# Four graph layers in one kernel: border, layer order and query/key stacks rearranged

## What is computed

```python
# layer 0: mean over neighbours
agg = (adj @ x) / maximum(adj.sum(-1), 1e-6);  y0 = relu(concat([x, agg]) @ W.T)
# layer 1: attention-like transition, two hops
e = leaky_relu(sj[None, :] + si[:, None] + ab, 0.2);  a = adj * exp(e)
T = a / (a.sum(-1) + 1e-12);  y1 = relu(sum_k (T^k x) @ Wk[k] + bk[k])   # k = 0, 1, 2
# layer 2: three graph convolutions
h = relu(adj' @ (x @ W1) + b1); h = relu(adj' @ (h @ W2) + b2); y2 = adj' @ (h @ W3) + b3
# layer 3: 8 heads of 32, scores multiplied by 2 * adj before the softmax
s = (q @ k.T) * 32 ** -0.5 * (adj + adj);  y3 = softmax(s) @ v @ Wo.T + bo
# after each layer: x = layernorm(x + y)
```

## Time and profile before

| what | value |
|---|---|
| median of 3 runs | 3148.42 us |
| profiled execution | 3147.59 us |
| its span, first to last instruction | 3145.7 us |
| granted TensorE clock, mean | 0.993 |
| TensorE (PE) busy | 3023.7 us |
| DVE, ACT, POOL busy | 2083.8, 1724.0, 453.5 us |
| DMA, mean over the span | 75 GB/s |

### The profile page before, as it was taken

One profiled execution on the slowest core, in us unless ns is written; L12 is line 12 of the kernel. 1 busy time (PEld: TensorE's weight loads), 2 busy tenths in 40 slices (PEclk: granted clock), 3 DMA queues, 4 the chain that ended last, 5 costly groups with the idle time before them and its releaser, 6 DMA issues.

```text
span 3145.7 us, 71077 instructions
## 1 busy us (share of the span) xinstructions
PE 3023.7 (96%) x28188; PEld 2644.0 (84%) x28188; DVE 2083.8 (66%) x4020; ACT 1724.0 (55%) x3048; POOL 453.5 (14%) x1666
## 2 busy tenths in 40 slices
PE   6999999999999999999999999999999999999999
PEld 6988789887898778987789877898778987789877
DVE  5637976379762797627975289753887438874387
ACT  3525854258552684426844278542784327853377
POOL 0101211012110122101221012111121111211112
PEclk9999999999999999999999999999999999999999
DMA  5122131121321213202133021330213302133110
GB/s 218 36 72 69 45 145 54 57 70 45 142 77 37 66 52 135 90 28 66 49 135 108 11 72 42 135 108 14 68 51 125 108 14 72 50 124 108 28 39 19
DMA packets 145271, 234.50 MB, mean 75 GB/s; under 512 B 12840, under 2 KB 113965, under 8 KB 144941
## 3 DMA queue, kind: packets, MB, share of 16 engines
q1 hardware_dynamic: 144940, 229.96, 22.5%
HBM read 120.86 MB, written 83.89 MB: 65 GB/s over the span
## 4 chain that ended last, share of the span: by engine, by line
PE 80%; DVE 10%; ACT 3%; issue 2%; SPq 2%; POOL 2%; DMA 0%; DVEq 0%; POOLq 0%; ACTq 0%
PE ps L725 15%; PE ps L497 15%; PE ps L499 14%; PE ps L498 14%; PE ps L715 9%; PE ps L743 7%; DVE rsum L1280 2%; PE ps L598 2%; SPq L400 1%; PE ps L587 1%; PE ps L756 1%; DVE ev L1379 1%; PE ps L555 1%; DVE t_lo L1210 1%; POOL rstd L461 1%
## 5 line engine op out<-in xcount | busy, mean ns | idle before, releaser
L1466 DVE CUSTOM_DVE_ANT_0 r<-ps,adjn 128x1024 f32<-128x1024 f32 x512 | 620.7, 1212 | 19.5 <-DVE xr L1502 10.3
L1141 ACT ACTIVATE r<-r,nmax 128x1024 f32<-128x1024 f32 x512 | 584.9, 1142 | 23.0 <-POOL nmax L489 22.6
L497 PE MATMUL ps<-u_hi,t_hi 128*128 128x256 f32 x2048 | 589.9, 288 | 5.8 <-DVE u_lo L1190 4.8
L499 PE MATMUL ps<-u_hi,t_lo 128*128 128x256 f32 x2048 | 579.2, 283 | 0.0
L498 PE MATMUL ps<-u_lo,t_hi 128*128 128x256 f32 x2048 | 578.8, 283 | 0.0
L725 PEld LDWEIGHTS ps<-ident,r 128*128 128x128 f32 x4096 | 462.5, 141 | 115.4 <-issue 77.6
L725 PE MATMUL ps<-ident,r 128*128 128x128 f32 x4096 | 536.7, 274 | 7.3 <-DVE pt L1482 6.9
L1482 DVE COPY pt<-ps 128x512 f32<-128x512 f32 x512 | 352.9, 689 | 92.6 <-PE ps L725 75.0
L497 PEld LDWEIGHTS ps<-u_hi,t_hi 128*128 128x128 f32 x2048 | 391.2, 191 | 14.3 <-DVE t_lo L1190 7.7
L907 ACT ACTIVATE pt<-ps 128x512 f32<-128x512 f32 x512 | 304.0, 594 | 175.8 <-PE ps L725 161.9
L498 PEld LDWEIGHTS ps<-u_lo,t_hi 128*128 128x128 f32 x2048 | 391.1, 191 | 0.0
(11 more groups left out here) (162 smaller groups left out, 5233.9 us busy)
## 6 DMA issues: line engine op xcount, KB each, us to landing
adjn<-in_adj SPq DMA_DIRECT2D x64, 512.0 KB, 3.4
t_spill<-t_hi SPq DMA_DIRECT2D x64, 512.0 KB, 4.5
t_spill<-t_lo SPq DMA_DIRECT2D x64, 512.0 KB, 5.3
t_hi<-t_spill SPq DMA_DIRECT2D x32, 1024.0 KB, 5.3
t_lo<-t_spill SPq DMA_DIRECT2D x32, 1024.0 KB, 8.0
xn<-in_x SPq DMA_DIRECT2D x16, 512.0 KB, 4.5
x_spill<-xn SPq DMA_DIRECT2D x64, 128.0 KB, 1.7
q_stack<-u_hi SPq DMA_DIRECT2D x64, 128.0 KB, 2.4
```

Of the source, the lines that this page charges most:

```text
L497: pe.matmul(dst, a_hi, b_hi, start=first, stop=False, skip_group_check=check)
L499: return pe.matmul(dst, a_lo, b_hi, start=False, stop=last, skip_group_check=check)
L1141: act.activation(r[:, s % RSLOTS, :], r[:, s % RSLOTS, :], ACT.Exp, bias=nmax[:, s % 4:s % 4 + 1], accum_out=prow[:, qt % 2, h:h + 1]).the ...
L1466: dve.tensor_tensor_reduce(out=r[:, s % RSLOTS, :], in0=ps[:, 2 * (s % 2):2 * (s % 2) + 2, :].rearrange("p a c -> p (a c)"), in1=adjn[:, q ...
```

## The change

It has four parts.

1. *Border.* The first halves of block columns 0 to 3 of the next adj are transposed inside the loop of the element before: 8 transposes ahead of the last context group, 8 behind it. Their copies are put into the lists of ACT and DVE at the loop's end; one DVE piece stands between the last output's sum and its statistics. `spread_denominators` of the last tile comes earlier, the last context group uses another PSUM bank, and the last tile's `c_f`, `c_hi`, `c_lo` are made in two halves. The `g` projections alternate one by one with the adj columns.
2. *Degrees.* One reduction before the border, three ahead of layer 0, four between its tiles; the reciprocals in two halves.
3. *Layer 1.* `v` pairs 0 to 2 move ahead of the late x transposes and of `s_j(1)`, pair 3 behind the first alpha transpose; DVE makes both parts of all four; ACT writes the first half of `sj_row`; two of the `s_i` move down. The own part runs two tiles ahead in the second hop.
4. *Stacks.* Only heads 0 and 1 are stacked by TensorE, and not their second query halves: 6 copies. All else is moved by transfers of 32 partitions x 2 KB, query or key and half each by itself: per element 78. The order of the projections is changed to suit. The last projection comes behind `scores(0)`. `scores(u)` of heads 2 to 7 waits for the transfers of its head, `scores(32)` for the second query halves. The copies to `pt` wait in steps.

The diff, cut to what decides:

```diff
+    PLACED = 2
+    COPIES = [(h, m, half) for m, half in ((1, 0), (0, 0), (1, 1)) for h in range(PLACED)]
-    QK = [(1, 0, 0), (1, 1, 0), (0, 0, 0), (0, 1, 0), (1, 0, 1), (1, 1, 1), (0, 0, 1), (0, 1, 1)]
+    QK = [(0, 1, 0), (0, 0, 0), (1, 1, 0), (1, 0, 0), (0, 1, 1), (1, 1, 1), (0, 0, 1), (1, 0, 1)]
...
+        P_RING = ([(pt_0, k) for k in (2, 0, 6, 4, 3)] + [(pt_1, k) for k in range(6)] +
+                  [(pt_0, 1), (pt_0, 5), (pt_2, 0), (pt_2, 1)])
...   SyncE
-                for g in range(G):
-                    rows = slice(HD * g, HD * (g + 1))
-                    for n in range(2):
-                        if g == 0:
-                            sp.wait_ge(pr_free, nth(b, PR_UNITS, pr["qk", (1, n, 1)] + 1))
-                        at = slice(n * N, (n + 1) * N)
-                        hi, lo = f32(u_hi[rows, at]), f32(u_lo[rows, at])
-                        stack = q_stack if n == 0 else k_stack
-                        for part, src in enumerate((hi, hi, lo) if n == 0 else (lo, hi, hi)):
-                            sp.dma_start(f32(stack[HD * part:HD * (part + 1), G + g, :]), src).then_inc(stacked[g], 16)
+                def moved(h, m, half, signal):
+                    src_rows, at = slice(HD * (h % G), HD * (h % G + 1)), slice(half * 512, (half + 1) * 512)
+                    stack = (q_stack, k_stack)[m]
+                    for part, lo in enumerate((0, 0, 1) if m == 0 else (1, 0, 0)):
+                        sp.dma_start(f32(stack[HD * part:HD * (part + 1), h, at]),
+                                     f32(qk_place((h // G, m, half), lo)[src_rows, :])).then_inc(signal, 16)
...
+                part_done((0, 0, 0))
+                first_halves(range(PLACED, G))
+                part_done((1, 0, 0))
+                first_halves(range(G, G + 1))
+                part_done((0, 1, 1))
+                key_halves(range(PLACED, G))
+                first_halves(range(G + 1, H))
+                part_done((1, 1, 1))
+                key_halves(range(G, H))
+                part_done((1, 0, 1))
+                for g in (1, 0):
+                    for h in range(G * g, G * (g + 1)):
+                        moved(h, 0, 1, queries_in[g])
...   TensorE, scores
+                if u < PLACED:
+                    copied(b, len(COPIES) - PLACED + u)
+                elif u < H:
+                    wait_first(pe, b, (u,))
+                    wait_keys(pe, b, (u,))
+                if u == H * TPH:
+                    wait_queries(pe, b, 0)
+                    wait_queries(pe, b, 1)
...   TensorE, query/key phase
+                qk_part(4)
+                for n in range(2 * PLACED):
                     stack_copies(b, n)
+                qk_part(5)
+                for n in range(2 * PLACED, 3 * PLACED):
+                    stack_copies(b, n)
+                qk_part(6)
                 scores(b, 0)
+                qk_part(7)
...   TensorE, end of the loop
+                    if s in (UNITS + 1, UNITS + 5) and b + 1 < B:
+                        for j in ((0, 1) if s == UNITS + 1 else (2, 3)):
+                            transpose_adj(b + 1, j, 0)
...   TensorE, second hop
+                own_part(0)
+                own_part(1)
                 for t in range(NT):
                     row_product(b, t, AF_P2)
+                    if t + 2 < NT:
+                        own_part(t + 2)
...   ScalarE, loop
+                        if u == 0:
+                            wait_first(act, b, range(G, H))
+                        if 2 * u + 1 == 11:
+                            wait_queries(act, b, 1)
+                        if 2 * u + 1 == 13:
+                            wait_queries(act, b, 0)
...   VectorE, border, layer 0 and loop
-                for j in range(NT):
-                    dve.tensor_reduce(rsum[:, j:j + 1], adjn[:, j, :], AX.X, ALU.add).then_inc(deg_sum, 1)
+                degree(b, range(1, TPH))
+                inverse_degrees(b, 0)
...
+                    if t < TPH:
+                        degree(b, (TPH + t,))
...
+                        if s == 0:
+                            wait_first(dve, b, range(PLACED, G))
+                        if s == 1:
+                            wait_keys(dve, b, range(PLACED, G))
...
+                        if u == 0:
+                            wait_first(dve, b, range(G, H))
+                        if u == 2:
+                            wait_keys(dve, b, range(G, H))
+                        if 2 * u == 12:
+                            wait_queries(dve, b, 1)
+                        if 2 * u == 14:
+                            wait_queries(dve, b, 0)
```

More of the change, by code:

```diff
@@ L51, in build_program @@
     adj_units = lambda *js: sum([halves_of("adj", j) for j in js], [])
-    TP_L0 = adj_units(0, 1) + x_units(0, 0) + adj_units(2, 3) + x_units(0, 1) + adj_units(4, 5, 6, 7)
+    TP_L0 = ([("adj", j, half) for half in range(HALVES) for j in range(TPH)] + x_units(0, 0) + adj_units(4, 5) +
+             x_units(0, 1) + adj_units(6, 7))
     AL = [(0, t) for t in range(TPH)] + [(1, t) for t in range(TPH)] + [(2, t) for t in range(TPH, NT)]
@@ new lines, in first_halves, with key_halves @@
+                def first_halves(heads):
+                    for h in heads:
+                        for m in range(2):
+                            moved(h, m, 0, first_in[h - PLACED])
+                def key_halves(heads):
+                    for h in heads:
+                        moved(h, 1, 1, keys_in[h - PLACED])
+                part_done = lambda part: sp.wait_ge(pr_free, nth(b, PR_UNITS, pr["qk", part] + 1))
+                part_done((0, 0, 0))
+                first_halves(range(PLACED, G))
@@ L950, in x_late_transposed, with adj_transposed @@
                     copy(dst, src).then_inc(tp_hi, 1)
-            def adj_transposed(b, layer, j):
-                for half in range(HALVES):
-                    n = tp_a(layer, j) + half
-                    act.wait_ge(tp_full, nth(b, TP_UNITS, n + 1))
-                    copy(t_hi[:, j, half * 512:(half + 1) * 512], tp_bank(n)).then_inc(tp_hi, 1)
+            def adj_transposed(b, js, halves=range(HALVES)):
+                for j in js:
+                    for half in halves:
+                        n = tp["adj", j, half]
+                        act.wait_ge(tp_full, nth(b, TP_UNITS, n + 1))
+                        copy(t_hi[:, j, half * 512:(half + 1) * 512], tp_bank(n)).then_inc(tp_hi, 1)
             def rows_from_pr(b, name, pairs=range(PAIRS)):
@@ L1047, in _ @@
                 al_transposed(0, 0)
-                rows_from_pr(b, "v", range(2, 3))
                 exponential(0, 2)
@@ L1203, in x_late_transposed, with adj_transposed, degree, inverse_degrees @@
                     rest(lo, src, hi, tp_free)
[L1205 to L1211 removed]
+            def adj_transposed(b, js, halves=range(HALVES)):
+                for j in js:
+                    for half in halves:
+                        n = tp["adj", j, half]
+                        at = slice(half * 512, (half + 1) * 512)
+                        dve.wait_ge(tp_hi, nth(b, TP_UNITS, n + 1))
+                        rest(t_lo[:, j, at], tp_bank(n), t_hi[:, j, at], tp_free)
+            def degree(b, js):
+                for j in js:
+                    dve.wait_ge(adj_in[j], nth(b, 16, 16))
+                    dve.tensor_reduce(rsum[:, j:j + 1], adjn[:, j, :], AX.X, ALU.add).then_inc(deg_sum, 1)
+            def inverse_degrees(b, half):
+                rows, n = slice(TPH * half, TPH * (half + 1)), (TPH + 1) * half + TPH
+                dve.wait_ge(deg_sum, nth(b, NT + 2, n))
+                dve.tensor_scalar(rsum[:, rows], rsum[:, rows], EPS_DEG, None, ALU.max).then_inc(deg_sum, 1)
+                dve.wait_ge(deg_sum, nth(b, NT + 2, n + 1))
+                dve.reciprocal(rdeg[:, rows], rsum[:, rows]).then_inc(deg_ready, 1)
             def rows_from_pr(b, name, u0, pairs=range(PAIRS)):
```

374 lines of the change are left out of this document (207 added, 167 removed).

## The result

The changed kernel takes 3283.6 us in the median of 4 runs (3282.7 to 3284.5); the kernel before, on the same chip, 3148.7 (3145.5 to 3149.6). The ratio is 1.0428, with a 95% interval of 1.0416 to 1.0441: 4.3% slower.

What follows compares the result with a forecast made beforehand. TensorE, busy 96% of the span, was taken to bound the kernel. 3147.6 + 122 (stack transfers and half clock) - 26 (border 8, degrees 9, layer 1 4, second hop 5) = 3243.6, given as 3243 us; range 3148 to 3270.

Steps and rivals of the forecast that it cites:

- Transfers: Query/key phase: 78 issues on SP, 0.635 us apart, make ACT's seventh `pt` copy come 14.6 us later per element.
- rival A: SP's stack transfers: small ones are cheap, step 0.32 to 0.36 us, so the time is 3076 us; chance 0.17.
- B: SP's stack transfers: an issue costs its shortest, step 0.55 us, last landing 8.1 us late, 3192 us; chance 0.15.
- Half clock behind the stall: TensorE after waiting for the last query transfers: 0.7 us lost per element, between nothing and 1.7.
- The border: Between elements: moved transposes gain 1.2 us net at 7 borders, 8 us in all; bounds 0.5 and 2.9.
- the gain from the half clock: At the border: if the half clock is gone too, 1.7 us, giving the upper bound of 2.9.
- Rival D: At the border: layer norm's chain takes all the 8 us gain, 3252 us; chance within 0.63 for the full step.
- Degrees: Layer 0: split reductions let DVE evacuate 5.7 us earlier, removing the wait for `ev`; 9 us gained, bounds 4 and 11.
- Layer 1 and second hop: Reordered work covers TensorE's waits for `xn` and `u_lo`: 4 us gained in layer 1, 5 in the second hop.
- rival C: Long issues (+8), full half clock (+8) and layer 1 losing (+9): 3269 us; chance within 0.63 for the full step.

Runs made afterwards that it cites:

- the last run: The version with three queues, with the 78 transfers dealt otherwise: SP 48, POOL 24, ACT 6; 3115.4 us, ratio 0.9895.
- the version with three queues: The kernel before with degrees, layer 1 and stacks, border as before, the 78 transfers issued by SP 45, ACT 15, POOL 18; 3110.0 us, ratio 0.9875.
- mended borders: The changed kernel without its stacks, with a degree sum and the fourth `t_lo` moved behind the last output's statistics on DVE; 3128.3 us, ratio 0.9937.

## Why the prediction was off

*Transfers: right in kind, nearly right in size.* One issue has a price of its own, 0.59, with the step near 0.635; start +5.2 and +5.2, last landing +56.5 and ACT's copy at +57.5 in the mean, `scores(4)` at +35.5 and +35.9. It should have been 14.6 us per element and was 15.5. The last issue starts 1.4 us late, by single long issues of up to 1.8 us, and lands 0.4 us sooner behind its issue than was taken. Rivals A and B fell: the median step of this form on SP is 0.63 us, and at any size tried the issue has a median of 0.59 to 0.60. Only single steps are as short as 0.56. The argument against A, that a first issue with nothing in flight has the full price, was the right row to go by. The sentence of the Trainium skill weighed there ("SBUF — State Buffer", "The DMA setup-cost knee (why "@ 1 MiB" ≠ asymptote)") gives the sequencer and descriptor generation ~50 ns and a few hundred ns. The prediction worked out rival A's 3076 from some 0.36 us of that, which is too little for a transfer from SBUF to SBUF on this queue: 0.59 us is gone at the issue. With DRAM at one end it is 0.42. Its advice to make few and large transfers fits the half-bytes run: with the same 78 transfers, half the bytes gave only 5 us.

*Half clock behind the stall: the term was too small.* 0.7 us per element was taken, between nothing and 1.7. Measured from the seventh to the last `pt` copy: 2.0 in the mean, 1.3 to 2.7 by element. The bound of 1.7 came from one border stall of the old kernel; here TensorE stood still several times (2.3, 1.4, 8.9 and 5.8 us in the element shown), and the half clock lasted up to 7.0 us behind the last of them. Transfers and clock together are 17.5 us per element by the trace, 140 in all; the run with the stacks alone has 144. Against the 122 of the forecast that is 22 of the 40 us by which it was off, about 7 by the transfers and 10 by the clock; the other 4 or 5 lie outside this stretch and are not taken apart.

*The border: the step that failed, with the wrong sign.* Expected 8 us gained, measured 19.5 lost: 27 us of the error. Three terms of it failed. The gain of 1.0 for halved pieces and an earlier `rbc` did not come, since DVE reaches `c_f` late: from DVE's last `pt` copy to the first matmul of the last output it is 6.7 us in the run without the stacks, 5.5 with the old border. The price of one `t_lo` in the chain, 0.69, was too low: the list of DVE has two `t_lo` and a degree sum ahead of `c_f`, 2.5 us, to which the prediction gave no price; it named the degree sum at the border and never asked what is queued behind it. And the gain from the half clock that was held possible became a loss: behind the longer stall three of seven borders of that run had twice the time at half clock. The waits of the alternated `g` projections for `xt_lo` and `u_lo` (7.5 and 6.3 us) were not foreseen either. Rival D, "the layer norm's chain takes all of it", stopped at a gain of zero, and it was DVE's list and not the layer norm's chain: moving two of its pieces gave 14 us back.

*Degrees:* 9 us expected, 12 measured. The wait for `ev` is gone as said. *Layer 1 and second hop:* 4 + 5 expected, 13 measured; the feared loss by DVE's two more copies did not come. The first is just above its bound of 11, the second within its bounds; together they were 7 us too low.

*The sum:* +22 (stacks and clock), +27 (border), -7 (layers) make +42, for a difference of 3283.6 - 3243 = 41.

*The range.* Its upper end was rival C, in which long issues, the half clock and layer 1 went to their bad ends and the border kept its gain; even the border's own lower bound was 0.5 us of gain. A part that adds work to an engine's list inside the critical chain needs a bound below zero. That the direction came out right is no luck, since the queue's step and the engine that waits were the forecast ones; that the miss is only 1.3% is in part, since the layers' 7 us offset some of it.

## What to carry to other kernels

A queue that issues transfers is an engine with a price per instruction: before splitting transfers, multiply their number by the step between two issues in the trace and see who waits for the last one; the bytes come second. Work moved ahead of a stall must be placed by each engine's list, behind what the chain needs and into the idle time that the timeline shows: the same two pieces, moved down DVE's list, gave 14 us. And a stall of TensorE can cost more than its length: 2 to 6 us of standing still mostly brought 3.4 to 7 us at half clock behind it, 1.2 to 2.7 us of time, and sometimes nothing.

## What the runs showed of the hardware

- An issue on SP costs 0.59 to 0.60 us for every transfer from SBUF to SBUF tried (16 to 128 rows, 32 to 128 KB), 0.42 to 0.43 for 64 KB to or from DRAM; the same SBUF to SBUF form costs 0.61 on ACT's queue and 0.50 on POOL. That rows and bytes change nothing, and the ends of the transfer do, I had not expected.
- Three queues at once are not three times as fast: while POOL and ACT both issued, SP's issues took 0.71 us in the mean of the last run, with single ones of 0.79 and 0.84. Which resource they share was not tried.
- POOL's last drain, for which the end of the program waits, took 0.3 us without transfers issued by POOL, 2.5 with 144 of them and 6.7 to 6.9 with 192; only the last made the program longer, by 4 us.
- The lower clock level (1.2 GHz) followed most of the stalls read here, for 3.4 to 7.0 us behind them, but not all: it stayed away behind 1.9 and 3.4 us of standing still in two elements of the version with three queues, and at two mended borders (1.9 us). In that version it cost 1.0 us per element in the mean (TensorE waited 2.3 us there, 18.1 in 8), and 2.0 in the changed kernel with its several stalls.
